# Plain step numbers in the walk tables of a four-layer graph network, and one semaphore per walk for gathered tiles

## The reference: what is computed

```
h = relu(_layernorm(x)); x = x + L0(h)    # two graph convolutions with degree norms
h = relu(_layernorm(x)); x = x + L1(h)    # mean of neighbours, concatenated, one product
h = relu(_layernorm(x)); x = x + L2(h)    # two sage convolutions, 128 -> 256 -> 128
h = relu(_layernorm(x)); x = x + L3(h)    # edge MLP over h[src], h[dst], weight; segment sum; node MLP; layer norm
```

## Time and profile before

| | |
|---|---|
| median of 3 runs | 5151.64 us |
| profiled execution, first to last instruction | 6457.2 us |
| of it ahead of walk 0 | 1142 us |
| PE busy | 4407.5 us (68%) |
| DVE busy | 3589.5 us (56%) |
| ACT busy | 3052.6 us (47%) |
| POOL busy | 3067.8 us (48%) |

### The profile page before, as it was taken

How to read it: one execution, slowest core, us unless ns; L and a number is a source line. 1 busy time by engine, 2 the same in 40 slices (tenths; PEclk the granted TensorE clock), 3 DMA queues, 4 the chain that set the end, 5 groups by cost and what they waited for, 6 DMA issues and landing times. The chain is left out here.

```text
span 6457.2 us, 132161 instructions
## 1 busy us (share of the span) xinstructions
PE 4407.5 (68%) x23072; PEld 3228.9 (50%) x23073; DVE 3589.5 (56%) x12501; ACT 3052.6 (47%) x6864; POOL 3067.8 (48%) x3248
## 2 busy tenths in 40 slices
PE   7755555677657877577758999777771566666557
PEld 2333333566656655444436777566661444444345
DVE  9865555444436655466645665466661445455446
ACT  7533333444435555455545665355550334344335
POOL 0154445455545553545535555355545545554541
PEclk9877787777778998899989999899995767777778
DMA  0022222444434444466656787567762444444444
GB/s 18 10 62 66 66 67 72 128 153 154 146 110 149 152 141 135 158 211 215 215 170 214 241 250 242 169 227 231 235 226 86 133 127 141 131 140 133 130 130 140
DMA packets 613683, 956.80 MB, mean 148 GB/s; under 512 B 100096, under 2 KB 255888, under 8 KB 613584
## 3 DMA queue, kind: packets, MB, share of 16 engines
q1 hardware_dynamic: 494848, 746.65, 34.7%
q0 software_dynamic: 100672, 181.64, 11.8%
q10 hardware_dynamic: 18064, 27.47, 1.2%
HBM read 517.00 MB, written 438.38 MB: 148 GB/s over the span
## 5 line engine op out<-in xcount | busy, mean ns | idle before, releaser
L1045 PE MATMUL banks<-M,OH 128*128 x7840 | 1323.0, 319 | 654.8 <-issue 597.2
L588 POOL DMA_INDIRECT M<-table_a,six x1176 | 1117.8, 950 | 903.2 <-PE banks L1045 357.4
L1045 PEld LDWEIGHTS banks<-M,OH 128*128 128x128 f32 x7840 | 1148.7, 215 | 758.3 <-issue 739.2
L681 ACT ACTIVATE AG<-banks x1176 | 635.0, 591 | 1240.0 <-remote 954.3
L588 POOL DMA_INDIRECT M<-table_b,six x784 | 767.6, 979 | 627.0 <-PE banks L1042 208.5
L578 POOL DMA_INDIRECT edges_by_block<-pack,pos_i x392 | 376.5, 961 | 679.7 <-DVE pos_i L1325 558.7
L588 POOL DMA_INDIRECT M<-table_pairs,six x392 | 393.2, 1003 | 572.7 <-DVE ES L1581 451.3
L1441 DVE TENSOR_TENSOR OH<-banks,dstrel 128x1024 f32<-128x1024 f32 x392 | 478.3, 1221 | 221.7 <-remote 190.6
L681 ACT ACTIVATE HT<-banks 128x512 f32<-128x512 f32 x588 | 348.4, 593 | 513.2 <-remote 416.4
L699 ACT ACTIVATE HO<-H,BI,SC 128x128 f32 (+1 forms) x1176 | 485.3, 485 | 133.8 <-issue 73.4
L681 ACT ACTIVATE T<-banks 128x512 f32<-128x512 f32 (+1 forms) x686 | 355.0, 532 | 312.6 <-remote 124.3
(11 more groups left out here) (319 smaller groups left out, 8716.4 us busy)
## 6 DMA issues: line engine op xcount, KB each, us to landing
XZ<-state SPq DMA_DIRECT2D x490, 256.0 KB
table_a<-T SPq DMA_DIRECT2D x294, 256.0 KB
state<-T SPq DMA_DIRECT2D x294, 256.0 KB
state<-H SPq DMA_DIRECT2D x196, 256.0 KB
own_products<-T SPq DMA_DIRECT2D x98, 512.0 KB
table_pairs<-T SPq DMA_DIRECT2D x98, 512.0 KB
M<-messages SPq DMA_DIRECT2D x98, 512.0 KB
XZ<-in_x SPq DMA_DIRECT2D x194, 256.0 KB
```

The lines of the kernel that those rows point to most:

```text
L588: nc.gpsimd.indirect_dma_start(out=M[:, slot, :], out_offset=None, in_=table, in_offset=bass.IndirectOffsetOnAxis(ap=idx, axis=0)).then_in ...
L681: return nc.scalar.activation(dst_, src_, ACT.Copy)
L1045: last = mm(banks[:, ds(sums_at[k], P)], OH[:, b * US + k, :], source[:, ds(rows_at[k], P)], start=False, stop=False, skip_group_check=True)
```

## The change

A row of the table holds 19 numbers in place of 16: the last tile of the window plus one, 8 tile offsets, 8 sum offsets, 2 fresh-bank offsets, each by itself. A walk loads only the part that it uses: walks 0, 1, 2 and 4 all 19, walk 3 the last 10, walk 5 the last 18; ACT in walk 3 loads the first 9 in place of 16. `tiles_ready` becomes six semaphores, one a walk. `tab_p` and `tab_a` become partitions 0 and 32 of one tensor. The start stage makes the tables with three instructions fewer on DVE.

```diff
-STEPW = 2 * US
+STEPW = 2 * US + 3
+ROWS_AT, SUMS_AT, FRESH_AT = 1, US + 1, 2 * US + 1
...
-        tab_p = sb("tab_p", [1, WINS, STEPW], I32)
-        tab_a = sb("tab_a", [1, WINS, 4], I32)
+        tab_pa = sb("tab_pa", [33, WINS, STEPW], I32)
+        tab_p = tab_pa[0:1, :, :]
+        tab_a = tab_pa[32:33, :, 0:4]
...
-        tiles_ready = sem("tiles_ready"); win_done = sem("windows_done"); oh_ready = sem("onehots_ready")
+        tiles_ready = [sem(f"tiles_ready{k}") for k in range(6)]; win_done = sem("windows_done"); oh_ready = sem("onehots_ready")
...
+        def window(eng, w, lo, hi):
+
+            return list(nc.values_load_multi_w_load_instructions(
+                tab_p[0:1, ds(w, 1), lo:hi].rearrange("o w k -> o (w k)"), engines=[eng.engine], min_val=0, max_val=RING * P,
+                skip_runtime_bounds_check_because=why)[1])
...
-                    pool.sem_inc(tiles_ready, GC)
+                    pool.sem_inc(tiles_ready[ph], GC)
...
-                act.wait_ge(tiles_ready, ((v[15] >> 16) & 511) + (TILES * 3 + 1))
+                act.wait_ge(tiles_ready[3], v[0] & 511)
...
-                    rows_at = [... for x in v[0:8]] if ph != 3 else None
-                    sums_at = [... for x in list(v[8:13]) + [x & 2047 for x in v[13:16]]]
-                    fresh_at = [... nc.s_assert_within(x >> 16, 0, 3 * W4, ...) for x in (v[14], v[13])]
+                    lo = {3: SUMS_AT, 5: ROWS_AT}.get(ph, 0)
+                    v = [None] * lo + window(pe, w, lo, STEPW)
+                    rows_at = [... for x in v[ROWS_AT:SUMS_AT]] if ph != 3 else None
+                    sums_at = [... for x in v[SUMS_AT:FRESH_AT]]
+                    fresh_at = [... for x in v[FRESH_AT:]]
...
-                        pe.wait_ge(tiles_ready, ((v[15] >> 16) & 511) + (TILES * ph + 1))
+                        pe.wait_ge(tiles_ready[ph], v[0] & 511)
...
-            v.tensor_scalar(t16[:, :], by_win(t_i[:, :])[:, :, US - 1], 16, None, ALU.logical_shift_left)
+            for tab in (tab_p, tab_q):
+                v.tensor_scalar(tab[:, :, 0], by_win(t_cl[:, :])[:, :, US - 1], 1.0, None, ALU.add)
...
-            link(v.tensor_tensor(tab_p[:, :, 2 * US - 1], tab_p[:, :, 2 * US - 1], t16[:, :], ALU.bitwise_or))
...
-            link(v.tensor_scalar(high[:, :, :], bank_i[:, 0:2 * WINS].rearrange("o (w k) -> o k w", k=2), 16, None, ALU.logical_shift_left))
             for tab in (tab_p, tab_q):
-                for k in range(2):
-                    link(v.tensor_tensor(tab[:, :, 2 * US - 2 - k], tab[:, :, 2 * US - 2 - k], high[:, k, :], ALU.bitwise_or))
+                v.tensor_copy(tab[:, :, FRESH_AT:STEPW], bank_i[:, 0:2 * WINS].rearrange("o (w k) -> o w k", k=2))
...
-                dve.wait_ge(tiles_ready, c * GC + (TILES * 5 + GC))
+                dve.wait_ge(tiles_ready[5], c * GC + GC)
```

More of the change, by code:

```diff
@@ L223, in program @@
         t_i = tmp("t_i", [1, STEPS], I32); b_i = tmp("b_i", [1, STEPS], I32)
-        t16 = tmp("t16", [1, WINS], I32); b15_i = tmp("b15_i", [1, STEPS], I32)
+        b15_i = tmp("b15_i", [1, STEPS], I32)
         half_i = tmp("half_i", [1, 2 * WINS + 2], I32); bank_i = tmp("bank_i", [1, 2 * WINS + 2], I32); slot_f = tmp("slot_f", [1, 2 * WINS + 2]); wrap = tmp("wrap", [1, 2 * WINS + 2])
-        high = tmp("high", [1, 2, WINS], I32)
         m_f = tmp("m_f", [1, STEPS])
@@ L830, in step_tiles @@
                 w = 2 * i + b
[L831 to L834, removed]
-                act.wait_ge(tiles_ready, ((v[15] >> 16) & 511) + (TILES * 3 + 1))
+                v = window(act, w, 0, SUMS_AT)
+                rows_at = [nc.s_assert_within(x, 0, (RING - 1) * P, skip_runtime_bounds_check_because=why) for x in v[ROWS_AT:]]
+                act.wait_ge(tiles_ready[3], v[0] & 511)
                 stand(act)
@@ L1019, in do @@
                     w = 2 * i + b
[L1020 to L1025, removed]
+                    lo = {3: SUMS_AT, 5: ROWS_AT}.get(ph, 0)
+                    v = [None] * lo + window(pe, w, lo, STEPW)
+                    rows_at = [nc.s_assert_within(x, 0, (RING - 1) * P if ph < 5 else (US - 1) * P, skip_runtime_bounds_check_because=why) for x in v[ROWS_AT:SUMS_AT]] if ph != 3 else None
+                    sums_at = [nc.s_assert_within(x, 0, 15 * P, skip_runtime_bounds_check_because=why) for x in v[SUMS_AT:FRESH_AT]]
+                    fresh_at = [nc.s_assert_within(x, 0, 3 * W4, skip_runtime_bounds_check_because=why) for x in v[FRESH_AT:]]
                     need(pe, ev_act, w + (WINS * ph - 1))
@@ L1371, in _ @@
             v.tensor_scalar(tab_t0[:, 0:WINS], by_win(t_i[:, :])[:, :, 0], 7, None, ALU.logical_shift_left)
-            v.tensor_scalar(tab_p[:, :, 0:US], by_win(t_i[:, :]), RING - 1, 7, ALU.bitwise_and, ALU.logical_shift_left)
-            v.tensor_scalar(tab_q[:, :, 0:US], by_win(m_f[:, :]), float(P), None, ALU.mult)
-            v.tensor_scalar(t16[:, :], by_win(t_i[:, :])[:, :, US - 1], 16, None, ALU.logical_shift_left)
+            v.tensor_scalar(tab_p[:, :, ROWS_AT:SUMS_AT], by_win(t_i[:, :]), RING - 1, 7, ALU.bitwise_and, ALU.logical_shift_left)
+            v.tensor_scalar(tab_q[:, :, ROWS_AT:SUMS_AT], by_win(m_f[:, :]), float(P), None, ALU.mult)
+            for tab in (tab_p, tab_q):
+                v.tensor_scalar(tab[:, :, 0], by_win(t_cl[:, :])[:, :, US - 1], 1.0, None, ALU.add)
             link(v.tensor_scalar(b15_i[:, :], b_i[:, :], 15, 7, ALU.bitwise_and, ALU.logical_shift_left))
-            v.tensor_copy(tab_q[:, :, US:2 * US], by_win(b15_i[:, :]))
-            link(v.tensor_copy(tab_p[:, :, US:2 * US], by_win(b15_i[:, :])))
-            link(v.tensor_tensor(tab_p[:, :, 2 * US - 1], tab_p[:, :, 2 * US - 1], t16[:, :], ALU.bitwise_or))
+            for tab in (tab_p, tab_q):
+                v.tensor_copy(tab[:, :, SUMS_AT:FRESH_AT], by_win(b15_i[:, :]))
             v.memset(half_i[:, 0:1], 0)
```

## The result

| | |
|---|---|
| changed kernel | 6011.08 us, median of 4 runs (6007.66 to 6012.05) |
| kernel before, in the same session | 5151.38 us, median of 4 runs (5147.08 to 5152.08) |
| ratio | 1.167, 95% interval 1.1655 to 1.1688 |
| predicted | 5074 us, range 5010 to 5165 |

A forecast was written before the change was run, and what follows sets the result against it. It took walks 0, 1 and 4 as bound by TensorE's stream just above POOL's gather floor, walks 2, 3 and 5 by other things; 39 + 20 + 18 + 1 = 78 us gained, 5152 - 78 = 5074 us, range 5010 to 5165.

The forecast's parts named there:

- Price of a longer load: TensorE's table load in walks 0, 1, 2 and 4: three more numbers cost 0.20 us, bounds 0 and 0.35.
- Slower: the longer load decides: Rival, chance 0.14: load at each window's head grows 0.35 us against 0.21 saved; walks 0, 1, 4 lose 41 us, 5193 us.
- Both signs of failure: Wrong if loads grow over 0.21 us and idle time before the opening product grows too, or walk 4's period doesn't fall.
- 1.52 us of slack: Walk 2: TensorE waits 1.52 us each window for ACT's HT, so a shorter stream gains 0, at most 62 us.
- Walks 3 and 5 were covered: Walk 3's stream lies beneath gapless products, walk 5's beneath POOL's gathers; both taken as 0 gain.
- 8 x 0.104 = 0.83 us: TensorE's stream, walks 0, 1, 2, 4: eight fewer register instructions at 0.104 us each; 0.63 us a window after the longer load.
- 39 + 20 + 18: Gains in us forecast for walks 4, 0 and 1, from 0.40, 0.20 and 0.18 us a window.
- The room: Window period above POOL's 5.0 us that a shorter stream could gain: walk 0 0.36 us, walk 1 0.18, walk 4 0.74.
- POOL's floor: Shortest window POOL's gathers allow, one each 1.25 us: 5.0 us in walks 0 to 4, 10.0 in walk 5.
- nothing gained: Rival, chance 0.20: register instructions cost half without recording, walks 0, 1, 4 already at POOL's period; 5152 us (5142 to 5162).
- 3989 + 1142 = 5131 of 5152 us: 98 windows at end-of-walk periods plus the start stage, as evidence that undisturbed windows are not slower in the profile.
- the start stage without weight: Table-making before the first window: fewer DVE instructions were forecast to save 1 us.

The follow-up runs named there:

- sems6: Kernel before with only six semaphores and the two tables joined in one tensor, rows still 16 packed numbers: 5151.51 us, ratio 0.9997.
- offset1: sems6 with its 16 packed numbers moved 4 bytes into rows of 80 bytes, so every load starts unaligned: 6059.56 us, ratio 1.177.
- aligned20: Changed kernel with its plain numbers reordered and one unused, rows of 20, every load aligned and a multiple of four numbers: 5155.13 us, ratio 1.0012.
- masks6: sems6 with six more register instructions a window behind the first step (needless masks), loads unchanged: 5194.00 us, ratio 1.0094.
- split16: sems6 with its 16 packed numbers reordered and loaded as 8 and 8, the second behind the fourth step: 5163.32 us, ratio 1.0041.
- split20: Changed kernel with plain numbers in aligned rows of 20, loaded as 12 and 8, the second behind the fourth step: 5147.81 us, ratio 0.9999.

## Why the prediction was wrong

**The step that failed: "Price of a longer load".** It took 59 to 69 ns a number from loads of 4 and of 16 numbers and made the three more 0.20 us, with bounds of 0 and 0.35. All the rows behind it were aligned loads of whole fours, so they gave a quarter of the price of a four, and no row showed a single number. The trace of the kernel before held one. SyncE loads one number at a time from `tab_s`:

```profile
L313 SPq TENSOR_LOAD <-tab_s x684: 2/272/857, 1143.7 to 6451.6; - x171
```

The median is 0.27 us for one number, beside 0.31 for four on ScalarE. As an estimate, three numbers at that price are 0.8 us, past the bound. Measured: a further aligned four costs 1.357 - 1.101 = 0.256 us; three single ones at the end of an aligned load 1.827 - 1.101 = 0.73 us, already beyond the bound; and with the start off a multiple of 16 bytes 19 take 4.5 us, 3.4 more than 16 aligned, which is 0.24 us for each number. The prediction read the change from 16 to 19 as a longer load. It was above all a change of the rows' distance from 64 to 76 bytes, which puts three of four loads off a multiple of 16 bytes, and the prediction never mentions that.

The Trainium skill (Runtime: NRT & Kernel Launch, section "Instruction fetch mechanics") gives register loads of this kind about 200 ns a register even in bulk, from HBM. The tables here lie in SBUF; unaligned loads come near that figure (3.80/16 = 0.24 us), aligned ones are far below it (1.10/16 = 0.069), and here the measurement decides. An estimate by that figure would have made three more numbers 0.6 us, past the 0.21 us from which the slower rival decides.

**The rival that came true.** "Slower: the longer load decides", at the head of each window, is what happened, with 3.0 us in place of 0.35. Both signs of failure that the text named are there. Walk 4's period did not fall, and loads grew by more than 0.21 us and the idle time ahead of the opening product with them, from 426.5 us in sems6 to

```profile
L1031 PE MATMUL banks<-zero_h x588: 167/174/211, 857.8 to 5949.8; 128*128 128x1 f16 x196
its engine sat idle before it (us, times) until:
  issue: 1913.6, 698
```

which is 1487 us more (idle time here counts PE and its weight loads each). Walk by walk, from the starts of sems6 and of the changed kernel, the periods went from 4.98, 5.39, 7.27, 7.18, 5.96 and 11.17 us to 7.37, 7.62, 8.56, 7.30, 8.53 and 11.22. Times 98 that is 234, 219, 126, 12, 252 and 5 us, 848 of the 857 us between the spans. Walk 2, whose stream had 1.52 us of slack, lost once the load grew by 3.6. Walks 3 and 5 were covered, as forecast.

**The loss doubles back through TensorE's clock.** PE's timeline in walk 1 of the changed kernel, windows 41 and 43:

```profile
1901.40 0.60 PE L965 MATMUL banks<-ident,HO 128*128 128x128 f32 x4
1905.53 0.18 PE L1031 MATMUL banks<-zero_h 128*128 128x1 f16 x1 [3.52 <-issue]
1905.85 2.07 PE L1049 MATMUL banks<-M,OH 128*128 x8
...
1914.47 0.17 PE L1031 MATMUL banks<-zero_h 128*128 128x1 f16 x1 [1.18 <-issue]
1914.80 1.15 PE L1049 MATMUL banks<-M,OH 128*128 x8
```

Behind the gap of 3.52 us four steps take 2.07 us, and 1.15 behind the short one. The granted clock is 1.00 from 1898.0 to 1901.9 us, while TensorE is busy, 0.50 from 1905.5 to 1909.6, behind the gap, and 1.00 again from 1911.6. In the mean over this walk it is 0.84 of 2.4 GHz, and it was 0.97 in sems6 (views by stretch, changed kernel first; columns us, then busy us of PE, PEld, DVE, ACT, POOL, PEclk, DMA share, GB/s):

```profile
1595.00:2328.00 733.00, 552.73 (x3213) 460.29 (x3214) 429.34 (x1504) 364.62 (x843) 375.64 (x404) 0.84 0.44 134
```

```profile
1360.00:1880.00 520.00, 476.94 (x3217) 393.39 (x3218) 422.97 (x1506) 374.60 (x844) 375.11 (x405) 0.97 0.60 190
```

The same products kept TensorE busy for 553 us in place of 477. As an estimate, up to 76 of the 219 us that the walk lost are then products at the lower level (1.2 GHz); how much of this lies beneath other waits isn't known. Over the program PE's busy time is 4355 us against 4042 in sems6. That the lower clock is a consequence of the late loads and no cause of its own is shown by offset1, whose only difference is the start of the loads, and whose clock fell from 0.93 to 0.88 over the whole span.

**"8 x 0.104 = 0.83 us" was right as a price, wrong as a gain.** The two instructions ahead of the first step do what was forecast; weight loads of aligned20 in walk 4, beside the earlier trace rows:

```profile
3708.30 0.10 PEld L1031 LDWEIGHTS banks<-zero_h 128*128 128x128 f16 x1 [1.30 <-issue]
3708.63 0.97 PEld L1049 LDWEIGHTS banks<-M,OH 128*128 128x128 f32 x8 [0.23 <-issue]
```

They start 0.33 us apart (0.31 was forecast) in place of 0.52. But taking away the six behind the first step hardly shortens the steps. From the first step to the first dense product a window of walk 1 takes 1.90 us in aligned20 (1600.46 to 1602.36) and 1.95 in sems6, as above. So these six lay beneath the products, while six more (masks6) do not fit there; and the sum "39 + 20 + 18" had counted 0.62 us of them as time to be gained. With the load priced rightly nothing would have been left either: aligned20 is 4 us slower than before.

**The room was misread too.** Behind the last gathers walk 0 had a period of 5.36 us, from which I took 0.36 us of room; over the whole walk in sems6 it is 4.98, at POOL's floor of 5.0. TensorE's weight loads do stand idle there ahead of the opening one, for "issue", for 80 us in all, but POOL's gathers set the period all the same. In walk 1 TensorE is busy for 477 of 520 us, so its products and not its registers fill the period. Walk 4 has gaps of the kind in the earlier trace rows that POOL doesn't cover, 91 us in all, yet halving the load at its head (split16) left the walk's period at the 5.96 us of sems6. The rival "nothing gained" is what the repaired change does, though not for its reason (shorter slots without recording; in the profile of sems6, which ran at the timed pace, the two weight loads of walk 4 still start 0.52 us apart, at 3707.84 and 3708.36). The weak reading was to take six windows at the end of each walk, from a single execution, for the whole of it: the same six windows of walk 0 last 6.38 us each in sems6, because one of them lasts 12.2. And the sum that was to show that such windows are not slowed in the profile, 3989 + 1142 = 5131 of 5152 us, came out by luck: without the slowness the start stage is 859 us (sems6) and not 1142, the six periods are 41.95 us together and not 40.7, and some 180 us between the walks and behind the last one were left out.

The Trainium skill (NOTIFIC — the notification-queue block, section 7.1), on records holding back their producers, was used to argue that profiles run slow. The eleven later profiles have spans within 0.2% of their timed medians; they ran at the usual pace, and what slowed that one execution stays open. No run here is without trace records, so none shows what these cost.

**What was right**: six semaphores at 0, walks 3 and 5 covered, POOL's floor in walk 0 (in walk 5 the period is 11.17 us and not 10.0; eight gathers there take 11.4 us from 4500.20 to 4511.58 in sems6, with two copies of indices between them), the start stage without weight (the first load stands at 855.5 us, and at 859.0 in sems6).

## What to carry to other kernels

Before pricing a table in SBUF that an engine loads into registers, work out where each load starts: keep the rows' distance and every offset at a multiple of 16 bytes, and pad or reorder the fields until they are, since one number of padding was worth 786 us here, and eight instructions fewer a window some 11. A price per element taken from loads of one size and one alignment says nothing on another. Register instructions that an engine issues beneath its own products cost nothing as long as they fit there: six a window did here, and twelve did not.

## What the hardware showed

- Register loads from SBUF: 16 numbers 1.10 us from a multiple of 16 bytes and 3.80 us from 4 or 8 bytes past one; 20 aligned, 1.36; 19 aligned, 1.83; 12 and 8 aligned, 0.85 and 0.59 (shortest ones, split20); a single one, 0.27 (SyncE). ScalarE is alike: 1.02 us for 16 aligned, at least 3.43 in offset1. That fours are fetched together is the reading that fits all of these; the runs show the durations only.
- Aligned loads are stretched under load as well, for the same count: the median of 16 numbers is 1.11 us in walk 5 and 2.11 in walk 2 (sems6). No run here tells what they contend with.
- A gap in TensorE's work of 3.5 us was followed by products at the lower clock (0.50, from 1.00 before it): a late stream cost its delay here and then slower products.
